# A mixture-of-experts stage whose gathered rows are turned by VectorE in 32x32 blocks, after small moves between partitions, in place of four TensorE transposes per tile

## The reference, cut to what matters

```python
scores = jax.nn.softmax(x @ gate_w.T, axis=-1)          # x: 2048 tokens x 512, 16 experts
topk_w, topk_ids = lax.top_k(scores, 6)
combine = ...                                            # weight of each token for each expert
def body(acc, ew):                                       # once per expert
    w13_e, w2_e, c_e = ew                                # 704 x 512, 512 x 352
    g, u = jnp.split(x @ w13_e.T, 2, axis=-1)
    return acc + c_e[:, None] * ((jax.nn.silu(g) * u) @ w2_e.T), None
out = ... + _swiglu(x, sw13, sw2)                        # shared expert, inner width 704
x = x + tanh(g_ffn) * out
```

## Time and profile before

| | us |
|---|---|
| median of 3 runs | 1429.51 (1429.09 to 1432.42) |
| the profiled execution, own time | 1428.72 |
| its span, first to last instruction | 1426.5 |
| TensorE busy in the span | 1342.8 |
| POOL, DVE, ACT busy in the span | 948.6, 785.2, 730.5 |

### The profile page before, as it was taken

One profiled execution on the slowest core, in us unless ns is written; L12 is line 12 of the kernel. 1 busy time (PEld: TensorE's weight loads), 2 busy tenths in 40 slices (PEclk: granted clock), 3 DMA queues, 4 the chain that ended last, 5 costly groups with the idle time before them and its releaser, 6 DMA issues.

```text
span 1426.5 us, 31834 instructions
## 1 busy us (share of the span) xinstructions
PE 1342.8 (94%) x8480; PEld 1208.7 (85%) x8481; DVE 785.2 (55%) x1364; ACT 730.5 (51%) x1317; POOL 948.6 (66%) x671
## 2 busy tenths in 40 slices
PE   6898998998898899999999999999999999999996
PEld 2676787887888799999999999999999998999995
DVE  6889898898999854653333333333333333333331
ACT  5899897898889464343332333323333333333321
POOL 0589899998998757887456665566645666646632
PEclk8899999998999999999999999999999999999998
DMA  4121123122241454645455535555445544455432
GB/s 138 38 75 31 54 68 102 66 93 69 76 160 68 135 123 103 146 81 141 84 144 143 132 62 146 140 144 142 105 94 139 143 134 101 102 146 133 76 67 36
DMA packets 65042, 149.13 MB, mean 105 GB/s; under 512 B 16976, under 2 KB 17616, under 8 KB 62656
## 3 DMA queue, kind: packets, MB, share of 16 engines
q0 software_dynamic: 31024, 62.10, 22.8%
q1 hardware_dynamic: 33392, 81.21, 17.3%
q10 hardware_dynamic: 560, 4.98, 0.9%
HBM read 101.50 MB, written 48.99 MB: 105 GB/s over the span
## 4 chain that ended last, share of the span: by engine, by line
PE 63%; DVE 3%; issue 2%; DVEq 1%; ACT 1%; POOL 1%; ACTq 0%; POOLq 0%
PE bank L1719 19%; PE bank L1699 18%; PE bank L1700 17%; PE bank L1687 3%; PE bank L1710 3%; DVE hs L1172 1%; PE bank L1604 1%; PE bank L1590 1%; PE bank L1602 1%; DVEq L1375 0%; POOL hc L949 0%; ACT ah L862 0%; DVE sc L1226 0%; PE bank L1665 0%; DVEq L1369 0%
## 5 line engine op out<-in xcount | busy, mean ns | idle before, releaser
L949 POOL TENSOR_TENSOR hc<-hs,crow 128x512 f32<-128x512 f32 x254 | 322.4, 1305 | 87.3 <-DVE hs L1172 81.5
L1699 PE MATMUL bank<-w,xh 128*128 (+1 forms) x1088 | 366.3, 338 | 6.2 <-DVE am L1393 2.9
L1700 PE MATMUL bank<-w,xh 128*128 (+1 forms) x1088 | 351.1, 323 | 0.0
L1015 POOL DMA_INDIRECT out_x<-ys,aid x104 | 169.8, 1633 | 271.3 <-issue 213.6
L1172 DVE TENSOR_TENSOR_SCAN hs<-dA,bank 128x512 f32<-128x512 f32 x256 | 295.6, 1208 | 46.2 <-PE bank L1604 28.8
L1719 PE MATMUL bank<-w,ah 128*128 (+1 forms) x816 | 264.8, 405 | 2.7 <-DVE al L1399 2.7
L1399 DVE TENSOR_TENSOR al<-bank,ah 128x384 fp32r<-128x384 f32 x136 | 75.9, 558 | 330.9 <-ACT ah L862 326.1
L1699 PEld LDWEIGHTS bank<-w,xh 128*128 128x128 f32 x1088 | 204.4, 188 | 26.0 <-issue 21.0
L1700 PEld LDWEIGHTS bank<-w,xh 128*128 128x128 f32 x1088 | 206.4, 190 | 4.1
L868 ACT COPY ys<-bank 128x512 f32<-128x512 f32 x136 | 79.8, 587 | 200.5 <-PE bank L1719 200.5
L1700 PE MATMUL bank<-w,xl 128*128 (+1 forms) x544 | 175.9, 323 | 0.0
(11 more groups left out here) (184 smaller groups left out, 2064.2 us busy)
## 6 DMA issues: line engine op xcount, KB each, us to landing
wraw<-in_wall SPq DMA_DIRECT2D x16, 2176.0 KB
crow<-c_rows SPq DMA_DIRECT2D x64, 256.0 KB, 3.3
xt<-token_rows_turned SPq DMA_DIRECT2D x32, 256.0 KB, 3.2
out_x<-ys POOLq DMA_DIRECT2D x32, 256.0 KB, 4.2
wraw<-in_wall ACTq DMA_DIRECT2D x2, 2176.0 KB
token_rows<-rowb SPq DMA_DIRECT2D x4, 1028.0 KB, 6.1
xrow<-in_x SPq DMA_DIRECT2D x4, 1024.0 KB, 7.5
out_x<-xrow SPq DMA_DIRECT2D x4, 1024.0 KB, 4.9
```

The source lines that it names most:

```text
L949: nc.gpsimd.tensor_tensor(hc[:, j, :], hs[:, j, :], crow[:, n % 4, :], ALU.mult).then_inc(hc_done, 1)
L1015: pool.indirect_dma_start(out_rows, bass.IndirectOffsetOnAxis(ap=aid[:, s:s + 1], axis=0), ys[:, s, :], None, bounds_check=TOKENS - 1, oob ...
L1699: nc.tensor.matmul(gate_bank[:, 0:I], xx, columns(w, off + ww + k * 2 * I, I), start=first, stop=last)
L1700: mm = nc.tensor.matmul(up_bank[:, 0:I], xx, columns(w, off + ww + k * 2 * I + I, I), start=first, stop=last)
```

## The change

Rows of a routed tile are no longer turned by TensorE. Instead:

1. `norm_chunk` stores the 512 features of a row in another order: the feature of block b (of 128), sub-block a (of 32) and place c goes to place (a, b, c). The gate's weights and the two shared weight sets are loaded in an order that fits (`fetch_turned`, five transfers in place of one).
2. SP gets a loop over the routed tiles (`move`): once the rows are gathered, 12 transfers, each of 32 partitions x 128 elements (512 B a partition), put the off-diagonal blocks of `xt` into `xs`. ScalarE copies the four diagonal ones (`keep`). In `xs`, four slots as well, each group of 32 partitions then has what a transpose within the group needs.
3. VectorE transposes the whole tile in 32x32 blocks from `xs` to `xq` (`turn`). `x_high` and `x_low` read `xq` in SBUF where they read bank 4 in PSUM.
4. `turn_x` is gone.
5. The raw weights get a second buffer (`second`; `raws` is a view over both). The transfer of set e+1 is issued by ScalarE inside `split_high(e)`; SP's `fetch` loop is gone.
6. `gather(t)` waits for the moves and the kept blocks of tile t-4, where it waited for the TensorE turn of that tile.

```diff
+            def move(t, s, m):                                   # SP
+                rows_in(sp, t, s, m, "sp")
+                apart(sp, xt_turned, t - 3, "sp")
+                for a in range(G):
+                    for g in range(G):
+                        if g != a:
+                            sp.dma_start(xs[a * Q:(a + 1) * Q, s, g * P:(g + 1) * P],
+                                         xt[g * Q:(g + 1) * Q, s, a * P:(a + 1) * P]).then_inc(moved[s], 16)
...
-            with sp.Fori(3, NX) as e:
-                fetch(e)
             sp.wait_ge(meta_ready, 2)
+            groups = routed_groups(sp)
+            with sp.Fori(0, groups) as i:
+                for k in range(4):
+                    move(4 * i + NS + k, k, i)
...
+            def keep(t, s, m=None):                              # ACT
+                rows_in(act, t, s, m, "act")
+                act.wait_ge(xt_turned, t - 3)
+                for a in range(G):
+                    own = nc.scalar.copy(xs[a * Q:(a + 1) * Q, s, a * P:(a + 1) * P], xt[a * Q:(a + 1) * Q, s, a * P:(a + 1) * P])
+                own.then_inc(kept, 1)
...
                     t, s = 4 * i + PEELED + k, (3 + k) % 2
+                    keep(t + 1, k, i)
                     a_high(t - 1, 1 - s)
                     x_high(t + 1, 1 - s)
...
-                nc.scalar.copy(columns(w, (e % 2) * 2 * WCOLS, mine), wraw[:, 0:mine]).then_inc(wh_done, 1)
+                nc.scalar.copy(columns(w, (e % 2) * 2 * WCOLS, mine), raws[:, bass.ds((e % 2) * FAR, mine)]).then_inc(wh_done, 1)
+                apart(act, wl_done, e, "act")
+                act.dma_start(raws[:, raw_at(e + 1)], wall[bass.ds((e + 1) % NX, 1)].rearrange("a p c -> p (a c)")).then_inc(raw_in, 16)
...
+            def turn(t, s4, m=None):                             # DVE
+                quarters_in(dve, t, s4, m, "dve")
+                dve.wait_ge(xh_done, t - 1)
+                nc.vector.transpose(xq[:, s4 % 2, :].rearrange("p (b g r) -> p g b r", g=G, r=Q),
+                                    xs[:, s4, :].rearrange("p (g b c) -> p g b c", g=G, c=Q)).then_inc(xt_turned, 1)
...
             def tile(t, s4, gathers=False, adds=False, m=None):
                 s = s4 % 2
+                if not (isinstance(t, int) and t + 1 < NS):
+                    turn(t + 1, (s4 + 1) % 4, m)
                 a_low(t - 1, 1 - s)
...
-            def turn_x(t, s, m=None):                            # PE
-                rows_in(pe, t, s, m, "pe")
-                at_least(pe, xl_done, t)
-                for k in range(HK):
-                    mm = nc.tensor.transpose(banks[4][:, k * P:(k + 1) * P], xt[:, s, k * P:(k + 1) * P], ident[:])
-                mm.then_inc(xt_turned, 1)
```

More of the change, by code:

```diff
@@ L67 @@
 EARLY = 4
+Q = 32
+G = P // Q
+MOVES = G * (G - 1)
+FAR = 33280
 PIECES = 8
@@ L356, in mamba_moe @@
         mem.close()
+        span = ExitStack()
+        raws = alloc(span, "raws", [P, FAR + WCOLS])
+        span.close()
         wraw = alloc(ctx, "wraw", [P, WCOLS])
@@ L388, in mamba_moe @@
         lasti = alloc(ctx, "lasti", [P, 1], I32)
-        fours = alloc(ctx, "fours", [P, 2], I32)
+        fours = alloc(ctx, "fours", [P, 3], I32)
+        second = alloc(ctx, "second", [P, WCOLS + 160])
+        xs = alloc(ctx, "xs", [P, 4, TC * P])
+        xq = alloc(ctx, "xq", [P, 2, H])
         lead_in = sem("lead_in")
@@ L447, in mamba_moe @@
         gathered = [sem(f"gathered{i}") for i in range(4)]
+        moved = [sem(f"moved{i}") for i in range(4)]
+        kept = sem("kept")
         zero_done = sem("zero_done")
@@ L506, in rows_in, with quarters_in, raws_of, fetch_turned @@
                 apart(eng, gathered[s], 16 * ((t - NS) // 4 + 1) if isinstance(t, int) else 16 * m + 16, who)
+        def quarters_in(eng, t, s, m, who):
+            apart(eng, moved[s], 16 * MOVES * ((t - NS) // 4 + 1) if isinstance(t, int) else 16 * MOVES * (m + 1), who)
+            apart(eng, kept, t + 1, who)
+        def raws_of(e):
+            return 16 * (G + 1) if isinstance(e, int) and e == 0 else 16 * (e + 1 + 2 * G)
+        def fetch_turned(eng, e):
+            for b in range(G):
+                eng.dma_start(wraw[b * Q:(b + 1) * Q, 0:W2AT].rearrange("c (a i) -> c a i", a=G),
+                              wall[e, :, b * 2 * I:(b + 1) * 2 * I].rearrange("(a c) i -> c a i", c=Q)).then_inc(raw_in, 16)
+            eng.dma_start(wraw[:, W2AT:WCOLS], wall[e, :, W2AT:WCOLS]).then_inc(raw_in, 16)
+        def raw_at(e):
+            return bass.ds((e % 2) * FAR, WCOLS)
         def routed_groups(eng):
@@ L1061, in _ @@
             pool.wait_ge(meta_ready, 2)
-            groups = routed_groups(pool)
-            with pool.Fori(0, groups - 2) as i:
+            looped = pool.value_load(fours[0:1, 2:3], min_val=E // 4 - 2, max_val=ROUTED // 4 - 2)
+            with pool.Fori(0, looped) as i:
                 for k in range(4):
                     t = 4 * i + NS + k
-                    gather(t + AHEAD, (k + AHEAD) % 4)
+                    gather(t + AHEAD, (k + AHEAD) % 4, i + (k + AHEAD - 4) // 4)
                     next_weights(t)
@@ L1072, in _ @@
                 if k + AHEAD < 8:
-                    gather(rest + k + AHEAD, (k + AHEAD) % 4)
+                    gather(rest + k + AHEAD, (k + AHEAD) % 4, looped + (k + AHEAD - 4) // 4)
                 next_weights(rest + k)
@@ L1727, in offset_of, with tile @@
                 return pe.snap((number + 1) % 2 * (2 * WCOLS))
-            def tile(t, s4, old, off, more=True, m=None, ahead=None):
+            def tile(t, s4, old, off, ahead=None):
                 s = s4 % 2
@@ L1767, in _ @@
                     apart(pe, wl_done, number, "pe")
-                    number = tile(4 * i + PEELED + k, (3 + k) % 4, old, off, True, i, 4 * i + PEELED + k + 1 if k < 3 else None)
+                    number = tile(4 * i + PEELED + k, (3 + k) % 4, old, off, 4 * i + PEELED + k + 1 if k < 3 else None)
                     old = off
@@ L1773, in _ @@
             apart(pe, wl_done, number, "pe")
-            tile(last, 3, old, off, False)
+            tile(last, 3, old, off)
             turn_a(last, 1)
```

54 lines of the change are left out of this document (30 added, 24 removed).

## The result

The changed kernel is slower: median 1584.7 us (1581.5 to 1592.3, 4 runs) against 1431.0 (1429.1 to 1433.4, 4 runs) for the kernel before on the same chip. The ratio is 1.108, 95% interval 1.104 to 1.113. The forecast was 1413 us with a range of 1394 to 1448, so it was wrong in sign. The profiled execution has a span of 1579.8 us, 153 more than before.

The account below looks back on a forecast made before the run. TensorE was taken to bound the kernel, busy 695 of 700 us. From 1428.7 us, -45.8 (transposes) + 4 (plain tiles) + 21 (first tiles) + 5 (start) = -16 gave 1413 us, range 1394 to 1448.

Parts of the forecast that it names:

- SyncE's queue: Rival: SyncE's issuing of 12 moves a routed tile becomes the bound; slower, 1434 to 1459 us; chance 0.17.
- deciding point (0.54): Issue time p in us at which SyncE's 12p + 0.4 a tile passes the mean tile of 6.88; 1434 us there.
- A: Named after the result, not forecast: the long low-part subtraction xl on VectorE, 7.5 to 9.0 us in 15 tiles.
- B: Named after the result: SyncE's queue of moves as the cause, issues 0.633 us apart, 8.24 us a tile.
- First tiles, +21: In 15 first tiles of an expert, copies and transpose ahead of al make down 1.6 us late, not 0.14: +21 us.
- Plain tiles, +4: In 89 plain tiles the new ScalarE and VectorE work fits; 0.05 us a tile, +4 us, ends 0 and +57.
- The start, +5: At the first routed tile, 12 moves issued in a row make TensorE stand once, +5 us.
- The removed term, -45.8: TensorE's four transposes in each of 104 routed tiles leave its row, 0.44 us a tile: -45.8 us.
- The transpose, 0.7: VectorE's block transpose of a routed tile takes 0.7 us, upper end 1.21.
- The clock: TensorE's granted clock in the routed stage was not expected below 1.00, since its waits stay short.

Follow-up runs that it names:

- e4: Kernel before, with x_low in routed tiles subtracting from a constant SBUF tile instead of PSUM bank 4 (low parts wrong); 1581.3 us, ratio 1.105.
- e1: Changed kernel with the block transpose written to PSUM, so x_low again reads one operand from PSUM; complete result; 1557.8 us, ratio 1.087.
- e6: e3 with four moves of 32 x 512 a tile and ScalarE's keep copies left out (routed output wrong); 1425.2 us, ratio 0.994.
- e3: Changed kernel with the block transpose written to PSUM and 6 moves a tile instead of 12 (routed output wrong); 1446.2 us, ratio 1.009.
- e7: e6 with the next tile's x_low ahead of take_weight and gather_ids on VectorE (routed output wrong); 1413.2 us, ratio 0.987.
- e10: TensorE turns every second routed tile, VectorE the rest with 12 moves each, x_low first for these, keep behind the silu; complete result; 1442.2 us, ratio 1.008.

## Why the prediction was wrong, step by step

- **The step that failed: reading `xq` in SBUF was costed at nothing.** The sum has no term for where `x_low` reads; the 0.69 us of its PSUM form were carried over. With both operands in SBUF it stands until GpSimd's 9.4 us subtraction is done, once per expert: 150 us by e4 alone, with TensorE's stretch at the lower clock in it. No rival had it. In the shared tiles `xl` reads `xt` and `xh`, both in SBUF, and took 0.69 us in the trace of before (mean of 32), where that subtraction doesn't run. But that profile did hold rows of such meetings, in the scan, and the prediction didn't read them: one VectorE product with both inputs in SBUF (`ex` and `rsm`, 128x64) took 3.57 us beside two-input work of GpSimd and ended 0.08 us behind it, where it takes 0.22 us beside GpSimd's transfers; and the sum `delta` with `du` (128x512) took 0.69 us alone and up to 1.76 beside GpSimd. VectorE, then GpSimd, of the kernel before:

```profile
434.24 3.57 DVE L1226 TENSOR_TENSOR sc<-ex,rsm 128x64 f32<-128x64 f32 x1
...
518.29 0.22 DVE L1226 TENSOR_TENSOR sc<-ex,rsm 128x64 f32<-128x64 f32 x1
```

```profile
433.89 1.38 POOL L958 TENSOR_TENSOR w<-wraw,w 128x544 fp32r<-128x544 f32 x1
435.20 2.53 POOL L949 TENSOR_TENSOR hc<-hs,crow 128x512 f32<-128x512 f32 x2
```

With these rows and GpSimd's 9.57 us beside VectorE's row, the wait could have been priced.

The Trainium skill ("SBUF — State Buffer", "SBUF: two separate sides") states this rule: a VectorE operation with two SBUF inputs and a GpSimd one that reads SBUF hold a port pair exclusively, and the later one blocks for the whole instruction. This case's traces agree: 7.6 us of `xl` beside 9.42 us on GpSimd in the changed kernel, 8.94 beside 9.39 in e4, and 0.69 in e1, where one input is in PSUM. One `xl` of e4 starts, by its record, 0.29 us ahead of GpSimd's subtraction and yet waits 10.21 us for its end; the records of GpSimd are rough. Weighed ahead of the forecast it would have been a slower rival of 15 x 8 = 120 us.

- **SyncE's queue.** Taken were 0.475 us an issue, from DRAM loads, and 6.1 us a tile. Measured were 0.633 and 8.2. This rival's mechanism was right and its deciding point (0.54) was passed; its 1459 us was priced at a pitch of 0.56. With A gone it makes e1's 1557.8. The pitch goes by issue, not bytes (0.633 us with 16 KB in the changed kernel, 0.634 with 64 KB in e6).
- **One does not add to the other.** A and B fill the same time: 27 + 9 for one edit each, 138.5 for both.
- **First tiles, +21.** The size held: 8.28 us a tile against 7.9, and 21.0 us between e3 and e6. The make-up did not: `keep` took 1.21 us and not 0.7, and without it these tiles lose their lateness although the transpose still stands ahead of `al`.
- **Plain tiles, +4.** Off by 8: VectorE's row binds in part of them (12 us between e6 and e7). The 2.11 us from `al` to `xl` is one tile's figure; in e6's tile it is 2.80. The loop's turn, for which the prediction took 0.35 us and no extra, costs 15.5 us more than before by e7.
- **The start, +5.** 9.4 of the 12.3 us: twelve moves in a row take 7.6 us rather than 5.7, and the second routed tile is late as well.
- **The removed term, -45.8.** Held: 6.29 against 6.73 us in e7.
- **The transpose, 0.7.** Held: 0.71.
- **The clock.** Expected 1.00 in the stage; from 700 to 1400 us it was 0.92, 0.91 with A alone (e4), 0.94 without A (e1) and 0.99 with neither A nor B (e3): a consequence of the waits.

The ledger from the changed kernel down: 1584.7, less 138.5 (A and B), less 21.0 (`keep`), less 12.0 (order) is 1413.2. TensorE's row alone would be 1431.0 less 45.8, 1385. Of the last 28 us the start holds 7.2 plus the 2.2 it should have saved. Of the rest, some 19 us, 15.5 are the loop's turns, and 2.3 were there ahead of the routed tiles.

## What to carry to other kernels

Before an operand moves from PSUM to SBUF, look for two-input VectorE operations on it and for long GpSimd work on SBUF that can meet them. Here one meeting cost up to the whole 9.4 us of GpSimd's instruction and then some 3.5 us of TensorE at its lower clock. A profile that holds such meetings shows them as instructions of one line and shape with very different durations. Price a queue by the issue pitch of its own kind of transfer, and a range by what happens just past the deciding point. When two causes fill the same time, undo both in one run as well as each alone: single edits showed 27 and 9 of 138 us.

## What was not expected of the hardware

- The block transpose of 128x512 float32 takes 0.71 us to SBUF, 0.73 to PSUM, and 1.12 when its input is read with a stride of four elements (e10).
- SyncE's transfers within SBUF are issued 0.633 us apart, with 16 KB and with 64 KB; its DRAM loads in the first row 0.475.
- After stands of 6.4 us (changed kernel) and 8.6 us (e4) TensorE's products ran at half clock (0.29 us apart, granted clock 0.50) for about 3.5 us.
- A two-input VectorE operation with both inputs in SBUF ended 0.55 to 0.57 us behind GpSimd's subtraction in all 30 meetings; with one input in PSUM it took 0.69 us beside it.
